# A recurrent (Mamba-style) layer with a quantized FFN on eight cores: the convolution of the next channel block is emitted four steps earlier, and the reload of the gated values gets one semaphore per half

## The chip, the cores and the metric

The kernel runs on all 8 cores of one Trainium2 chip. Each core computes 2 of the 16 sequences by itself; the cores share nothing but the weights they read. The metric is the device time of one execution, in microseconds (us), of the slowest core.

## What is computed

The input x is 16 sequences of 2048 tokens with 1024 channels, in float32. The reference, cut to what matters:

```python
xn = layernorm(x)
xp = xn @ in_proj_w.T + in_proj_b          # 1024 -> 2 * 2048
x1, x2 = split(xp, 2)
u  = silu(causal_depthwise_conv4(x1) + conv_b)
for t in range(2048):                      # per channel d, 16 states n
    h[d, n] = dA[d, n] * h[d, n] + dB[d, n] * u[t, d]
    y[t, d] = sum_n h[d, n] * C[d, n]
s = (y * silu(x2)) @ out_proj_w.T + out_proj_b
g = silu(ffn(xn))                          # silu(gate) * up, then down; hidden 3072, int weights / 127
out = x + s * g
```

## The kernel before

Everything is written out by hand: `build_schedule` appends each instruction to the list of its engine, with the semaphores that it waits for, and each engine runs its list in order. All matrix work is bf16, with PSUM tiles of 128x512. The work of one sequence (loop `u`) has these stages.

1. Layernorm of 16 tiles of 128 tokens, and transposes into `xnt` (channels on partitions, all 2048 tokens).
2. The scan stage: 16 channel blocks (loop `i`), each of 128 channels of the 2048. Each block has 16 steps (loop `n`, one for each state), and then a gate. A document-wide naming is used below: scan n, y n, piece g, unit.
   - Scan n (line 605, VectorE, `bfb<-aa,bfb`, 128x2048) runs the recurrence of state n over all tokens. It writes one of two buffers, so it waits until the y matmuls of step n-2 have read theirs. Behind it stands a small operation (line 613) that builds the diagonal weights C*dB of that state.
   - y n (line 625, TensorE) is 4 matmuls that add the state's part to `ps_y`, four PSUM banks that hold the block's sum. They wait for line 613 of their step.
   - The gate (line 640, VectorE) multiplies `ps_y` by silu(x2) when y 15 is done; SyncE then stores the result to `xg_spill` in DRAM (line 661).
   - Pieces 0 to 7 (`emit_ip_piece`, line 511) are the input projection of the next block, i+1, 8 matmuls each: pieces 0 to 3 give x1, 4 to 7 give x2. Pieces 0 to 5 stand behind y 1, 3, 5, 7, 9 and 11, pieces 6 and 7 behind the gate's place in the program, that is right behind y 15 on TensorE. ScalarE empties them (lines 521 and 532).
   - Three FFN units (`emit_f1`) a block: one ahead of scan 0, one behind y 6, one behind y 12. A unit is 8 transposes of its weight (line 155, emptied by ScalarE at line 162) and 16 matmuls (line 462, emptied at line 475). The one at the block's head comes with the 16 transposes of the next block's input weights (`emit_ip_slabs`), so 24 transposes stand ahead of its matmuls. A short product of VectorE (line 427) belongs to every second unit.
   - The convolution of block i+1 (`emit_conv`): 4 diagonal weights on VectorE (line 554), then 4 groups of 4 matmuls (line 571), emptied by ScalarE with silu (line 580) into the input of the next block's scans. It needs pieces 0 to 3. In the kernel before it is emitted behind y 13. The last block of a sequence (i = 15) has no next block and so neither pieces nor a convolution.
3. Two column halves of 1024 tokens (loop `cb`). In each, SyncE reads the gated values back with 32 DMAs of 128 KB (line 695), 16 for the first 512 columns (p = 0) and 16 for the second (p = 1). The output projection (line 719) has 8 output blocks m, and for each of them a group of 16 matmuls for p = 0 in `ps_a` or `ps_b` and one of 16 for p = 1. Then comes the down projection of the FFN (line 817), with the product and the sum of the outputs. In the second half the first FFN layer (48 units) runs ahead of the output projection.

All the groups of pieces, units, convolution and projections take the two PSUM tiles `ps_a` and `ps_b` in turn. The 48 units of the first half are just the three of each block, so nothing of the FFN is left between the last gate of a sequence and the first output projection. In this kernel one semaphore counts all reload DMAs, and each group of line 719 waits for the last of the 32:

```python
w = [fr, (ts, ev_t), ("qxg", lastl),
     ("sv", ev_g_done_v)]
```

Of the kernel before, what the change touches and what calls it, by code (L numbers as in the profile page):

```python
# [20 lines left out]
NI = DI // 128  # L21
# [11 lines left out]
RACE_CHECK = True  # L33

ENGS = ("sync", "gpsimd", "vector", "scalar", "tensor")
SEMS = ("q0", "qx0", "qx1", "qx2", "qx3", "qxg", "qxp", "qs",
        "qsx0",
        "qip0", "qip1", "qf0", "qf1", "qe0", "qe1", "qd0", "qd1",
        "sv", "ss", "st")
# [194 lines left out]
def build_schedule(sch, dr, sb, ps):  # L234
    op, val = sch.op, sch.val
    f32a, bfa, bfb = sb["f32a"], sb["bfa"], sb["bfb"]
# [5 lines left out]
    for nm_s, nm_d in (("b1s", "b1r"), ("convws", "convw"), ("convbs", "convb"),  # L242
# [6 lines left out]
                      inc="q0", inck=16)  # L249
# [57 lines left out]
    for u in range(BPC):  # L307
# [5 lines left out]
        for g in range(4):  # L313
# [61 lines left out]
            for jj in range(4):  # L375
# [3 lines left out]
                for dc in range(NK):  # L379
                    w = []  # L380
# [209 lines left out]
        for i in range(NI):  # L590
            uslot = bfb[:, 4096 + 2048 * (i % 2):4096 + 2048 * (i % 2) + 2048]
            if i + 1 < NI:
                emit_ip_slabs(i + 1)
            emit_f1(u, 0, 1)
            for n in range(NST):
                hs = bfb[:, 10240 + 2048 * (n % 2):10240 + 2048 * (n % 2) + 2048]
                dg = bfb[:, 2564 + 128 * (n % 2):2564 + 128 * (n % 2) + 128]
                if n >= 2:
                    ev_hfree = ev_dmm[(i, n - 2)]
                elif i > 0:  # L600
                    ev_hfree = ev_dmm[(i - 1, NST + n - 2)]
                else:
                    ev_hfree = bfb_free_st
                ev_scan[(i, n)] = op("vector",
                                     (lambda i, n, hs, uslot: lambda e: e.tensor_tensor_scan(  # L605
                                         hs,
                                         sb["aa"][:, 16 * i + n:16 * i + n + 1].broadcast_to([128, T]),
                                         uslot, 0.0, ALU.mult, ALU.add))(i, n, hs, uslot),
                                     waits=[("ss", ev_usilu[i]),
                                            ("st", ev_hfree)],  # L610
                                     inc="sv")
                ev_dg = op("vector",
                           (lambda i, n, dg: lambda e: e.tensor_scalar_mul(  # L613
                               dg, sb["idbs"][:],
                               sb["cbt"][:, 16 * i + n:16 * i + n + 1]))(i, n, dg),
                           inc="sv")
                lastd = None
                for pc in range(NPC):
                    w = []
                    if pc == 0:  # L620
                        w = [("sv", ev_dg)]
                        if n == 0:
                            w.append(("sv", ev_gate.get(i - 1, 0)))
                    lastd = op("tensor",
                               (lambda n, pc, dg, hs: lambda e: e.matmul(  # L625
                                   ps["y"][:, 512 * pc:512 * (pc + 1)], dg,
                                   hs[:, 512 * pc:512 * (pc + 1)],
                                   start=(n == 0), stop=(n == NST - 1)))(n, pc, dg, hs),
                               waits=w, inc="st" if pc == NPC - 1 else None)
                ev_dmm[(i, n)] = lastd  # L630
                if n % 2 == 1 and n <= 11 and i + 1 < NI:
                    emit_ip_piece(i + 1, n // 2)
                if n in (6, 12):
                    emit_f1(u, 0, 1)
                if n == 13 and i + 1 < NI:
                    emit_conv(i + 1)
            xgs = bfb[:, 16640:18688]
            sx2 = SX2_SLOT[i % 2]
            ev_gate[i] = op("vector",
                            (lambda xgs, sx2: lambda e: e.tensor_tensor(  # L640
                                xgs, ps["y"][:, :], sx2, ALU.mult))(xgs, sx2),
                            waits=[("st", ev_dmm[(i, NST - 1)]),
                                   ("ss", ev_x2evac[(i, NPC - 1)]),
                                   ("qsx0", ev_xgst.get(i - 1, 0))],
                            inc="sv")
            if DEBUG_TAPS and u == 0:
                op("sync",
                   (lambda i, uslot: lambda e: e.dma_start(
                       out=dr["t_u"][128 * i:128 * (i + 1), :], in_=uslot))(i, uslot),
                   waits=[("sv", ev_gate[i])], inc="q0", inck=16)  # L650
                op("sync",
                   (lambda i, sx2: lambda e: e.dma_start(
                       out=dr["t_sx2"][128 * i:128 * (i + 1), :], in_=sx2))(i, sx2),
                   waits=[("sv", ev_gate[i])], inc="q0", inck=16)
                op("sync",
                   (lambda i: lambda e: e.dma_start(
                       out=dr["t_hpp"][128 * i:128 * (i + 1), :],
                       in_=bfb[:, 12288:14336]))(i),
                   waits=[("sv", ev_gate[i])], inc="q0", inck=16)
            ev_xgst[i] = op("sync",  # L660
                            (lambda u, i, xgs: lambda e: e.dma_start(
                                out=dr["xg"][u, 128 * i:128 * (i + 1), :],
                                in_=xgs))(u, i, xgs),
                            waits=[("sv", ev_gate[i])],
                            inc="qsx0", inck=16)
            if i + 1 < NI:
                emit_ip_piece(i + 1, 6)
                emit_ip_piece(i + 1, 7)
# [5 lines left out]
        for cb in range(NCB):  # L674
# [8 lines left out]

            ev_sevac = {}
            ev_emm_last = 0
            lastl = None
            for p in range(2):
                pg = 2 * cb + p
                for k in range(NI):
                    w = []  # L690
                    if p == 0 and k == 0:
                        w = [("qsx0", ev_xg_all0), ("sv", ev_b_end_v),
                             ("st", ev_f2_mm_last)]
                    lastl = op("sync",
                               (lambda u, pg, p, k: lambda e: e.dma_start(
                                   out=bfb[:, 2048 + 8192 * p + 512 * k:
                                           2048 + 8192 * p + 512 * (k + 1)],
                                   in_=dr["xg"][u, 128 * k:128 * (k + 1),
                                                512 * pg:512 * (pg + 1)]))(u, pg, p, k),
                               waits=w, inc="qxg", inck=16)  # L700
            for m in range(8):
                ew = []
                if m == 0:
# [6 lines left out]
                for p in range(2):  # L710
                    idx, fr = rot.acquire()
                    psm = PSR[idx]
                    for k in range(NI):
                        w = []
                        if k == 0:
                            w = [fr, (ts, ev_t), ("qxg", lastl),
                                 ("sv", ev_g_done_v)]
                        lastm = op("tensor",
                                   (lambda m, p, k, psm, wst: lambda e: e.matmul(  # L719
# [186 lines left out]
```

How the kernel before makes its waits and increments, by code:

```python
                def f(eng):  # L71
                    for (w, fn, ih) in ops_:
                        for (h, v) in w:
                            eng.wait_ge(h, v)
                        ins = fn(eng)
                        if ih is not None:
                            assert ins is not None
                            ins.then_inc(ih[0], ih[1])
```

## Time and profile before

| | |
|---|---|
| runs of the kernel, two | 4256.11 and 4409.76 us, median 4332.93 us |
| profiled execution, its own time | 4262.4 us |
| its span on the slowest core (core 4) | 4260.9 us |
| spans of the eight cores | 4232.0 to 4260.9 us |
| TensorE matmuls, busy | 2921.0 us (69%) |
| VectorE busy | 2578.2 us (61%) |
| ScalarE busy | 1165.9 us (27%) |
| mean granted TensorE clock, core 4 | 0.869 |

The span is the time from the first to the last instruction of a core; the execution's own time is 1.5 us longer. Busy shares are means over stages: in the two scan stages VectorE is busy nearly all of the time, in the projections TensorE is. A granted clock of 1.00 is TensorE at 2.4 GHz, 0.50 is 1.2 GHz. A matmul's busy time in a timeline row includes the end of the pipeline, so a row of 8 matmuls of 128x512 shows 1.89 us where the next group starts about 1.7 us behind it.

### The profile page before, as it was taken

The page shows a single profiled execution, that of the slowest core. Times are in us where ns is not written, and L with a number is a line of the kernel's source. Part 1 is how long each engine was busy: PE and PEld are TensorE (multiplying, and loading weights), DVE is VectorE, ACT ScalarE, POOL GpSimd, SP SyncE. Part 2 cuts the span into 40 slices and gives each one's busy share as a digit, 9 for nine tenths or more (in the row PEclk, how much of TensorE's full clock was granted, in tenths as well). Part 3 has the DMA queues.
Part 4 walks back from the last instruction along what each step waited for, and adds up shares of the span by engine and source line. Part 5 has one row for each costly group of instructions (what it writes and reads, how often), then busy time and mean ns, then how long its engine had stood idle before and what let it go on. Part 6 is the DMA issues. An engine that isn't in the chain of part 4 may idle for free.

```text
span 4260.9 us, 40605 instructions; the slowest of 8 cores (4232.0 to 4260.9 us)
## 1 busy us (share of the span) xinstructions
PE 2921.0 (69%) x14080; PEld 1296.0 (30%) x14080; DVE 2578.2 (61%) x1507; ACT 1165.9 (27%) x1575; POOL 169.3 (4%) x324
## 2 busy tenths in 40 slices
PE   3666676677675687767736776776776756877777
PEld 1222222222222343333322222222222223433333
DVE  2999999999998010000129999999999980100001
ACT  6222222122121233432362222221221212334332
POOL 0000000000000000000000000000000000000000
PEclk9889889888887889999958888888888878999998
DMA  3111111111101436323231111111111014263322
GB/s 99 25 20 25 25 20 25 25 20 26 24 15 26 111 62 153 47 48 55 54 109 25 20 25 25 20 25 25 20 27 23 15 27 118 54 156 46 51 50 70
DMA packets 84574, 196.07 MB, mean 46 GB/s; under 512 B 10272, under 2 KB 27040, under 8 KB 84384
## 3 DMA queue, kind: packets, MB, share of 16 engines
q0 software_dynamic: 46080, 109.07, 16.0%
q1 hardware_dynamic: 38304, 84.40, 5.9%
q8 instruction: 127, 2.08, 0.2%
q14 instruction: 63, 0.52, 0.0%
HBM read 268.93 MB, written 33.55 MB: 71 GB/s over the span
## 4 chain that ended last, share of the span: by engine, by line
PE 35%; issue 27%; DVE 23%; ACT 10%; DMA 2%; SPq 1%; DVEq 0%; ACTq 0%; POOLq 0%
DVE bfb L605 19%; PE ps_a L462 7%; PE ps_b L462 6%; PE ps_a L817 5%; ACT bfa L162 4%; PE ps_b L817 4%; PE ps_y L625 3%; PE ps_a L719 3%; PE ps_b L719 3%; DVE bfb L613 2%; PE ps_a L511 2%; ACT bfb L162 2%; PE ps_b L511 2%; ACT f32a L336 1%; ACT s_sb L475 1%
## 5 line engine op out<-in xcount | busy, mean ns | idle before, releaser
L605 DVE TENSOR_TENSOR_SCAN bfb<-aa,bfb 128x2048 bf16<-128x2048 f32 x512 | 2261.0, 4416 | 114.7 <-PE ps_y L625 66.4
L625 PE MATMUL ps_y<-bfb 128*128 128x512 bf16 x2048 | 636.9, 444 | 595.9 <-DVE bfb L613 594.5
L462 PE MATMUL ps_a<-xnt,bfa 128*128 128x512 bf16 x1536 | 404.2, 411 | 247.3 <-ACT bfa L162 226.6
L759 DVE TENSOR_TENSOR bfb<-f32a,s_sb 128x1024 bf16<-128x1024 f32 x32 | 39.2, 1225 | 788.1 <-PE ps_t L155 597.3
L625 PEld LDWEIGHTS ps_y<-bfb 128*128 128x128 bf16 x2048 | 198.9, 107 | 978.2 <-issue 854.3
L462 PE MATMUL ps_b<-xnt,bfa 128*128 128x512 bf16 x1536 | 374.1, 387 | 43.0 <-ACT bfa L162 43.0
L427 DVE TENSOR_TENSOR bfa<-s_sb 128x1024 bf16<-128x1024 bf16 x96 | 65.9, 687 | 514.0 <-ACT s_sb L475 514.0
L162 ACT ACTIVATE bfa<-ps_t 128x1024 bf16<-128x1024 bf16 x320 | 319.0, 1019 | 201.7 <-PE ps_t L155 197.8
L511 PE MATMUL ps_a<-xnt,bfa 128*128 128x512 bf16 x1024 | 321.9, 471 | 2.6 <-ACT bfb L532 1.4
L511 PE MATMUL ps_b<-xnt,bfa 128*128 128x512 bf16 x1024 | 318.7, 467 | 0.0
L462 PEld LDWEIGHTS ps_a<-xnt,bfa 128*128 128x128 bf16 x1536 | 147.0, 102 | 438.7 <-issue 313.0
L475 ACT ACTIVATE s_sb<-ps_a,cnss 128x512 bf16<-128x512 f32 x192 | 131.9, 687 | 446.9 <-PE ps_a L462 444.5
L155 PE MATMUL ps_t<-idbs,bfa 128*128 128x128 bf16 x2560 | 191.4, 224 | 66.3 <-ACT bfa L162 36.6
L462 PEld LDWEIGHTS ps_b<-xnt,bfa 128*128 128x128 bf16 x1536 | 152.5, 100 | 237.2 <-issue 74.9
L817 PE MATMUL ps_a<-bfa,bfb 128*128 128x512 bf16 x768 | 196.8, 419 | 18.5 <-ACT bfb L162 18.5
L155 PEld LDWEIGHTS ps_t<-idbs,bfa 128*128 128x128 bf16 x2560 | 167.5, 100 | 127.3 <-issue 77.1
L719 PE MATMUL ps_a<-bfb,bfa 128*128 128x512 bf16 x512 | 125.6, 402 | 109.2 <-ACT bfa L162 62.5
L475 ACT ACTIVATE s_sb<-ps_b,cnss 128x512 bf16<-128x512 f32 x192 | 131.9, 687 | 248.3 <-PE ps_b L462 248.3
L511 PEld LDWEIGHTS ps_b<-xnt,bfa 128*128 128x128 bf16 x1024 | 121.2, 118 | 190.6 <-issue 121.6
L511 PEld LDWEIGHTS ps_a<-xnt,bfa 128*128 128x128 bf16 x1024 | 119.6, 117 | 186.0 <-issue 113.4
L817 PE MATMUL ps_b<-bfa,bfb 128*128 128x512 bf16 x768 | 171.0, 379 | 0.0
L532 ACT ACTIVATE bfb<-ps_a,b1s 128x512 bf16<-128x512 f32 x64 | 44.0, 687 | 405.6 <-PE ps_a L511 389.3
(60 smaller groups left out, 1786.3 us busy)
## 6 DMA issues: line engine op xcount, KB each, us to landing
f32a<-x SPq DMA_DIRECT2D x64, 512.0 KB, 7.1
bfa<-wg POOLq DMA_DIRECT2D x96, 256.0 KB, 3.6
bfa<-wu POOLq DMA_DIRECT2D x96, 256.0 KB, 3.6
bfb<-wd POOLq DMA_DIRECT2D x32, 768.0 KB, 7.0
bfa<-win POOLq DMA_DIRECT2D x64, 256.0 KB, 5.6
xg_spill<-bfb SPq DMA_DIRECT2D x32, 512.0 KB, 2.6
bfa<-wout POOLq DMA_DIRECT2D x32, 512.0 KB, 6.1
bfb<-xg_spill SPq DMA_DIRECT2D x128, 128.0 KB, 5.6
```

What stands on the lines that cost most here:

```text
L155: (lambda stage, bank, g0, j: lambda e: e.transpose(bank[:, 128 * j:128 * (j + 1)], stage[:, 128 * (g0 + j):128 * (g0 + j + 1)], self.idma ...
L162: (lambda wst, bank, g0, nb: lambda e: e.activation(wst[:, 128 * g0:128 * (g0 + nb)], bank[:, 0:128 * nb], AF.Identity))(wst, bank, g0, nb),
L427: (lambda mh, sl: lambda e: e.tensor_tensor(bfa[:, 8192 + 1024 * mh:8192 + 1024 * (mh + 1)], s_sb[:, 2048 * sl:2048 * sl + 1024], s_sb[:, ...
L462: (lambda wst, k, cb, p, psm: lambda e: e.matmul(psm[:, :], wst[:, 128 * k:128 * (k + 1)], xnt[:, 2048 * k + 1024 * cb + 512 * p: 2048 * k ...
L475: (lambda dst, psm, act: lambda e: e.activation(dst, psm[:, :], act, scale=sb["cnss"][:, 2:3]))(dst, psm, act),
L511: (lambda k, p, psm, wst: lambda e: e.matmul(psm[:, :], wst[:, 128 * k:128 * (k + 1)], xnt[:, 2048 * k + 512 * p:2048 * k + 512 * (p + 1)] ...
L532: (lambda p, mrow, psm, sx2: lambda e: e.activation(sx2[:, 512 * p:512 * (p + 1)], psm[:, :], AF.Silu, bias=sb["b1s"][:, mrow:mrow + 1]))( ...
L605: (lambda i, n, hs, uslot: lambda e: e.tensor_tensor_scan(hs, sb["aa"][:, 16 * i + n:16 * i + n + 1].broadcast_to([128, T]), uslot, 0.0, A ...
L613: (lambda i, n, dg: lambda e: e.tensor_scalar_mul(dg, sb["idbs"][:], sb["cbt"][:, 16 * i + n:16 * i + n + 1]))(i, n, dg),
L625: (lambda n, pc, dg, hs: lambda e: e.matmul(ps["y"][:, 512 * pc:512 * (pc + 1)], dg, hs[:, 512 * pc:512 * (pc + 1)], start=(n == 0), stop= ...
L719: (lambda m, p, k, psm, wst: lambda e: e.matmul(psm[:, :], wst[:, 128 * k:128 * (k + 1)], bfb[:, 2048 + 8192 * p + 512 * k: 2048 + 8192 * ...
L817: (lambda wst, k, p, psm: lambda e: e.matmul(psm[:, :], wst[:, 128 * k:128 * (k + 1)], bfa[:, 8192 + 1024 * k + 512 * p: 8192 + 1024 * k + ...
```

## The change

Two edits. The convolution of the next block is emitted behind piece 4 of step 9 in place of step 13, so that its 4 diagonal weights, 16 matmuls and 4 operations of ScalarE stand four steps earlier in their engines' lists. And the reload DMAs of p = 0 and of p = 1 count on semaphores of their own (`qxg`, `qxg2`); a group of matmuls of line 719 waits for the 16 of its own half alone. Their order on SyncE's queue is the same.

```diff
+SEMS = (..., "qxg", "qxg2", ...)
...
                 if n % 2 == 1 and n <= 11 and i + 1 < NI:
                     emit_ip_piece(i + 1, n // 2)
+                if n == 9 and i + 1 < NI:
+                    emit_conv(i + 1)
                 if n in (6, 12):
                     emit_f1(u, 0, 1)
-                if n == 13 and i + 1 < NI:
-                    emit_conv(i + 1)
...
-            lastl = None
+            lastl_p = [None, None]
...
-                    lastl = op("sync",
+                    lastl_p[p] = op("sync",
...
-                               waits=w, inc="qxg", inck=16)
+                                    waits=w, inc=("qxg" if p == 0 else "qxg2"),
+                                    inck=16)
...
-                            w = [fr, (ts, ev_t), ("qxg", lastl),
+                            w = [fr, (ts, ev_t),
+                                 (("qxg" if p == 0 else "qxg2"), lastl_p[p]),
                                  ("sv", ev_g_done_v)]
```

TensorE's list in the middle of block 2 of the first sequence, before: y 8 and y 9 (the row of 8), piece 4, y 10 and y 11, piece 5, y 12.

```order
L625 MATMUL ps_y<-bfb 128x512 x8
L511 MATMUL ps_a<-xnt,bfa 128x512 x8
L625 MATMUL ps_y<-bfb 128x512 x8
L511 MATMUL ps_b<-xnt,bfa 128x512 x8
L625 MATMUL ps_y<-bfb 128x512 x4
```

The same place in the changed kernel, where line 571 is the convolution:

```order
L625 MATMUL ps_y<-bfb 128x512 x8
L511 MATMUL ps_a<-xnt,bfa 128x512 x8
L571 MATMUL ps_b<-bfb 128x512 x4
L571 MATMUL ps_a<-bfb 128x512 x4
L571 MATMUL ps_b<-bfb 128x512 x4
L571 MATMUL ps_a<-bfb 128x512 x4
L625 MATMUL ps_y<-bfb 128x512 x8
L511 MATMUL ps_b<-xnt,bfa 128x512 x8
L625 MATMUL ps_y<-bfb 128x512 x4
```

The 16 matmuls of the convolution now stand between piece 4 and y 10, so that y 10 comes behind 24 matmuls instead of 8.

TensorE's list at the end of the same block, before: the unit behind y 12 (line 462), y 13, the convolution, y 14 and y 15, pieces 6 and 7.

```order
L462 MATMUL ps_a<-xnt,bfa 128x512 x8
L462 MATMUL ps_b<-xnt,bfa 128x512 x8
L625 MATMUL ps_y<-bfb 128x512 x4
L571 MATMUL ps_a<-bfb 128x512 x4
L571 MATMUL ps_b<-bfb 128x512 x4
L571 MATMUL ps_a<-bfb 128x512 x4
L571 MATMUL ps_b<-bfb 128x512 x4
L625 MATMUL ps_y<-bfb 128x512 x8
L511 MATMUL ps_a<-xnt,bfa 128x512 x8
L511 MATMUL ps_b<-xnt,bfa 128x512 x8
```

The same place in the changed kernel:

```order
L462 MATMUL ps_a<-xnt,bfa 128x512 x8
L462 MATMUL ps_b<-xnt,bfa 128x512 x8
L625 MATMUL ps_y<-bfb 128x512 x12
L511 MATMUL ps_a<-xnt,bfa 128x512 x8
L511 MATMUL ps_b<-xnt,bfa 128x512 x8
```

Between the unit and pieces 6 and 7 TensorE has only y 13, y 14 and y 15, one behind each scan. The last block of a sequence has the rows `x12` there in both kernels.

VectorE's list in the middle of that block, before: scan 9 to scan 11 (line 605), each with its diagonal of line 613.

```order
L605 SCALAR_TENSOR_TENSOR bfb<-aa,bfb 128x2048
L613 TENSOR_SCALAR bfb<-idbs,cbt 128x128
L605 SCALAR_TENSOR_TENSOR bfb<-aa,bfb 128x2048
L613 TENSOR_SCALAR bfb<-idbs,cbt 128x128
L605 SCALAR_TENSOR_TENSOR bfb<-aa,bfb 128x2048
```

The same in the changed kernel, where line 554 is the convolution's diagonals:

```order
L605 SCALAR_TENSOR_TENSOR bfb<-aa,bfb 128x2048
L613 TENSOR_SCALAR bfb<-idbs,cbt 128x128
L554 TENSOR_SCALAR bfb<-idbs,convws 128x128 x4
L605 SCALAR_TENSOR_TENSOR bfb<-aa,bfb 128x2048
L613 TENSOR_SCALAR bfb<-idbs,cbt 128x128
```

The four small operations stand ahead of scan 10 now, and no longer ahead of scan 14.

## Rows read from the trace of the kernel before

**Rows 1.** The costliest groups, shapes kept apart: the scans (busy us, mean ns | idle before).

```profile
L605 DVE TENSOR_TENSOR_SCAN bfb<-aa,bfb 128x2048 bf16<-128x2048 f32 x512 | 2261.0, 4416 | 114.7 <-PE ps_y L625 66.4 <-PE ps_t L155 24.3 <-ACT bfb L580 23.9
```

**Rows 2.** The table of waits: who waited for whom, us in total, times, longest.

```profile
DVE bfb L605 <- PE ps_y L625: 66.4, 30, 4.0
...
DVE bfb L640 <- PE ps_y L625: 46.9, 32, 2.3
PE ps_a L719 <- DMA bfb<-xg_spill: 46.7, 2, 23.7
```

**Rows 3.** Timeline of block 5, from scan 10 to y 10 (start, us, engine).

```profile
551.81 4.42 DVE L605 TENSOR_TENSOR_SCAN bfb<-aa,bfb 128x2048 bf16<-128x2048 f32 x1
...
552.04 1.86 PE L625 MATMUL ps_y<-bfb 128*128 128x512 bf16 x4 [3.45 <-DVE bfb L613]
...
553.70 3.62 PE L511 MATMUL ps_a<-xnt,bfa 128*128 128x512 bf16 x8
...
556.28 4.42 DVE L605 TENSOR_TENSOR_SCAN bfb<-aa,bfb 128x2048 bf16<-128x2048 f32 x1
...
557.11 1.36 PE L625 MATMUL ps_y<-bfb 128*128 128x512 bf16 x4
```

**Rows 4.** Stretches with granted clock: length, PE, PEld, DVE, ACT, POOL busy, PEclk, DMA share, GB/s.

```profile
552.00:557.50 5.50, 5.46 (x13) 1.90 (x14) 5.50 (x3) 0.03 (x1) 0.00 (x0) 0.50 0.00 0
571.80:580.80 9.00, 6.76 (x31) 2.75 (x30) 7.61 (x4) 3.33 (x5) 0.00 (x0) 1.00 0.00 1
...
1370.50:1374.90 4.40, 1.87 (x4) 0.44 (x4) 2.24 (x2) 0.00 (x0) 1.05 (x2) 0.50 0.06 7
```

**Rows 5.** Timeline of block 5, from the diagonals of the convolution to the gate.

```profile
569.72 0.73 DVE L554 TENSOR_SCALAR bfb<-idbs,convws 128x128 bf16<-128x128 bf16 x4
...
571.80 1.03 PE L625 MATMUL ps_y<-bfb 128*128 128x512 bf16 x4
...
572.66 1.03 PE L571 MATMUL ps_a<-bfb 128*128 128x512 bf16 x4
...
576.65 1.03 PE L625 MATMUL ps_y<-bfb 128*128 128x512 bf16 x4
...
579.55 1.02 PE L625 MATMUL ps_y<-bfb 128*128 128x512 bf16 x4 [1.88 <-DVE bfb L613]
...
580.82 2.29 DVE L640 TENSOR_TENSOR bfb<-ps_y,bfb 128x2048 bf16<-128x2048 f32 x1 [1.41 <-PE ps_y L625]
```

**Rows 6.** Timeline of block 15 of the first sequence, which has no convolution in its tail.

```profile
1366.07 1.02 PE L625 MATMUL ps_y<-bfb 128*128 128x512 bf16 x4 [0.39 <-DVE bfb L613]
...
1370.55 1.87 PE L625 MATMUL ps_y<-bfb 128*128 128x512 bf16 x4 [3.45 <-DVE bfb L613]
...
1372.66 2.29 DVE L640 TENSOR_TENSOR bfb<-ps_y,bfb 128x2048 bf16<-128x2048 f32 x1 [2.26 <-PE ps_y L625]
```

**Rows 7.** Timeline behind the gate of block 5: piece 6, FFN unit, third scan.

```profile
580.41 1.89 PE L511 MATMUL ps_a<-xnt,bfa 128*128 128x512 bf16 x8
...
588.22 3.33 PE L462 MATMUL ps_a<-xnt,bfa 128*128 128x512 bf16 x8 [1.48 <-DVE bfb L613]
...
594.49 4.42 DVE L605 TENSOR_TENSOR_SCAN bfb<-aa,bfb 128x2048 bf16<-128x2048 f32 x1 [1.82 <-PE ps_y L625]
```

**Rows 8.** Timeline behind the gate of block 4: piece 6, first y, third scan.

```profile
499.72 3.57 PE L511 MATMUL ps_a<-xnt,bfa 128*128 128x512 bf16 x8
...
514.25 1.89 PE L625 MATMUL ps_y<-bfb 128*128 128x512 bf16 x8
...
515.38 4.42 DVE L605 TENSOR_TENSOR_SCAN bfb<-aa,bfb 128x2048 bf16<-128x2048 f32 x1 [4.01 <-PE ps_y L625]
```

**Rows 9.** Timeline where the output projection begins, in the first and the second sequence.

```profile
1384.34 16.29 SPq L695 DMA_DIRECT2D bfb<-xg_spill  x32
...
1405.59 6.33 PE L719 MATMUL ps_a<-bfb,bfa 128*128 128x512 bf16 x16 [23.74 <-DMA bfb<-xg_spill]
...
3534.12 5.32 PE L719 MATMUL ps_a<-bfb,bfa 128*128 128x512 bf16 x16 [22.92 <-DMA bfb<-xg_spill]
```

More of the change, by code:

```diff
@@ L35 @@
 ENGS = ("sync", "gpsimd", "vector", "scalar", "tensor")
-SEMS = ("q0", "qx0", "qx1", "qx2", "qx3", "qxg", "qxp", "qs",
+SEMS = ("q0", "qx0", "qx1", "qx2", "qx3", "qxg", "qxg2", "qxp", "qs",
         "qsx0",
@@ L693, in build_schedule @@
                              ("st", ev_f2_mm_last)]
-                    lastl = op("sync",
[L695 to L699, printed above, removed]
-                               waits=w, inc="qxg", inck=16)
+                    lastl_p[p] = op("sync",
+                                    (lambda u, pg, p, k: lambda e: e.dma_start(
+                                        out=bfb[:, 2048 + 8192 * p + 512 * k:
+                                                2048 + 8192 * p + 512 * (k + 1)],
+                                        in_=dr["xg"][u, 128 * k:128 * (k + 1),
+                                                     512 * pg:512 * (pg + 1)]))(u, pg, p, k),
+                                    waits=w, inc=("qxg" if p == 0 else "qxg2"),
+                                    inck=16)
             for m in range(8):
```

## The prediction

> **What bounds the kernel now.** I read the groups of costly instructions first. The 512 scans take 2261.0 us, 4.416 each, and VectorE sits idle before them for 114.7 us in all [rows 1]. That is more than half of the span of 4260.9 us, so in the scan stages the scans are the bound, and only idle time of VectorE there can be won or added. The reader is to see three waits in the 114.7: 66.4 for y matmuls, and 24.3 and 23.9 that occur once each, at the head of each sequence. They sum to 114.6. So no scan within a sequence waits for the convolution's output (line 580): it is ready in time at step 13 already, and having it earlier buys nothing.
>
> The table of waits says how the 66.4 us fall: 30 times, 4.0 us at most, 2.2 on average [rows 2]. There are 30 blocks with a successor (15 in each sequence). By the timelines it is nearly always the third scan behind a gate, which must wait for y 0, and y 0 stands behind pieces 6 and 7, 24 transposes and a unit. The gates wait 46.9 us for y 15 in 32 times. The output projection waits twice for the reload, 23.7 us at most.
>
> Then I read timelines around one block with the granted clock beside them, since TensorE's list is what is moved. Three things are to be seen:
>
> - Where TensorE has had only a few matmuls behind each scan, it is slow when work comes: y 9 takes 1.86 us for 4 matmuls and piece 4 runs from 553.70 to about 557.1 [rows 3]; the clock in these 5.5 us is 0.50, TensorE at 1.2 GHz [rows 4].
> - With the convolution between y 13 and y 14, TensorE is busy for 6.76 of the 9.0 us ahead of the gate, the clock is 1.00 [rows 4], y 15 takes 1.02 us, and the gate waits 1.41 us [rows 5].
> - In block 15, which has no convolution there, the y 14 still takes 1.02 us, but y 15 takes 1.87 us at a clock of 0.50, and the gate waits 2.26 us [rows 4, 6]. It has the very order (y 13, y 14, y 15 in a row) that the change gives to the 30 other blocks.
>
> **The change part by part.**
>
> *The tail loses its matmuls.* Between the unit and the pieces there are now 12 matmuls spread over three scans. The nearest rows are those of block 15: 2.26 - 1.41 = 0.85 us more at each gate [rows 5, 6], on the path, since gate and scans follow each other on one engine. 30 x 0.85 = 25.5 us. The other end is 0, if in most blocks the unit and y 13 come late enough to keep the clock up to y 15. I take 25.5, since a row with the same order shows it.
>
> *Pieces 6 and 7 start at the lower clock.* They follow y 15 at once. At 2.4 GHz piece 6 shows 1.89 us and the third scan waits 1.82 us, although half of the unit is slow there [rows 7]. Where piece 6 began at the lower clock it took 3.57 us and the third scan waited 4.01 us, the longest of all [rows 8, 2]. If every block goes that way, the wait rises from the mean of 2.2 by 1.8, 30 x 1.8 = 54 us; if the clock is back as soon as the pieces start, it rises by 0. By the row of 5.5 us at 0.50, y 15 uses 1.7 of such a stretch and up to 3.8 are left for the pieces, which costs 1.9; some stretches will be shorter. I take 1.0 us a block, a little over the middle, 30 us. What hides nothing here: the two scans between gate and third scan (9.0 us) are already overrun by 2.2.
>
> *The convolution stands ahead of y 10.* Scan 12 writes the buffer that y 10 reads, so y 10 is due before it. Scan 10 starts at 551.81 in this block, now some 0.6 later because of the diagonals (0.73 us on VectorE, as long as they took ahead of scan 14, so no term of its own) [rows 3, 5]. Scan 12 is then due at 552.4 + 2 x 4.48 = 561.4, 4.48 being a scan with its issue (556.28 - 551.81) [rows 3]. TensorE: piece 4 gives way at 557.1, the 16 matmuls take 576.65 - 572.66 = 4.0 at 2.4 GHz [rows 5], so y 10 starts at 561.1, and a scan starts 1.13 behind the start of its y (515.38 - 514.25) [rows 8]: 562.2. Scan 12 would wait 0.8 us here. With the clock up from y 9 on, y 9 and piece 4 take half of the 5.06 us, y 10 starts at 558.6, and nothing waits. So the ends are 0 and 30 x 0.8 = 24 us. Only the blocks with a whole slow stretch before y 10 pay, and I take 0.3 a block, 9 us. The far end is a convolution wholly at 1.2 GHz, 4 us more, which the rows speak against: TensorE is busy without a break from y 9 on, and in the row y 10 at 557.11 is already faster (1.36 for 4) than y 9.
>
> *Other queues.* On ScalarE four operations move ahead of the emptying of piece 5 and of the unit; it is idle for most of a block, and the PSUM tiles alternate as before. The x1 columns that the convolution reads come from piece 3, two steps earlier. SyncE and GpSimd keep their order. These I cost at 0; the cover is ScalarE's idle time.
>
> *The reload.* The 32 loads are issued over 16.29 us; the matmuls start at 1405.59, after 23.74 us idle [rows 9]. The sixteenth is issued about 8 us before the last, so the p = 0 group can start near 1397.4. It took 6.33 us (5.32 in the second sequence), part of it at the lower clock [rows 9]. The p = 1 group still needs the last load, so it begins at about 1405.5 in place of some 6 us later. The gain is at most what p = 0 took, 6.3 + 5.3 = 11.6 us for both. The pause before p = 1 may leave the clock down; its 16 matmuls would then lose about 16 x 0.21 = 3.4 us each time, by the two speeds of piece 6, and 4.8 us stay. I take 8. In the second column half the matmuls wait for no load, the table has two such waits alone [rows 2], so 0 there.
>
> *The sum.* 25.5 + 30 + 9 - 8 = 56.5 us on the profiled execution's own time of 4262.4 us: 4319 us, +1.3%. That execution agrees with the faster of the two runs shown (4256.11), while their median, 4332.93, lies between two runs that are 3.6% apart. My number is to be read beside 4256 to 4262.
>
> A rule that speaks against the clock terms: the Trainium skill, "TensorE: Matmul & The Clock Gate", section on the HAM clock gate (Part 1), says that for modelling the ramp penalty is below 1% of a typical kernel's span. By it, as an estimate, the two clock terms together would be under 42.6 us and the time 4306 us at most. The trace goes against it as a rule for this kernel: the waits of the third scans alone are 66.4 us, 1.6% of the span, and the spread from 1.82 to 4.01 among them follows the clock of the pieces.
>
> **The rivals.**
>
> *A: the lower clock in full, in every block.* Mechanism: every gate comes after a lean tail, y 15 and the pieces all run at 1.2 GHz, and scan 12 waits in every block as well. 25.5 + 54 + 24 - 5 = +98.5 us, 4361 us, +2.3%. For it: both blocks 15 look alike, and the phases of blocks repeat, so that one bad pattern can stay. Against it: time at the lower clock spent on y 15 can't be spent on the pieces too, and in this trace most blocks have their pieces at 2.4 GHz. It is slower than before beyond 2% from about 3.1 us a block on (85 + 8 = 93 over 30).
>
> *B: the tail keeps its clock.* Without the convolution at 13 the unit behind y 12, which itself may be slow and end late, covers enough of the tail. Then only the reload counts: 4262.4 - 8 = 4254 us. For it: y 14 of block 15 is still fast. Against it: y 15 of block 15 is not.
>
> *C: the pattern of clock falls well.* The matmuls of y 9, piece 4, convolution and y 10 are one busy run, and blocks shift so that the units behind the gate run fast. If the third scans waited for nothing: -66.4 - 8 = -74 us, 4188 us, -1.7%. Against it: y 0 still has 24 transposes and 32 matmuls before it, and the one mechanism that the change touches there works the other way. Beyond 2% it would need the gates' wait to shrink too, which they can't, since y 15 follows scan 15.
>
> **How the numbers follow.** Forecast 0.55, A 0.25, B 0.15, C 0.05. The time is that of the forecast, 4319 us. The range: B gives 4254, with 11.6 us of gain for the reload 4250; A gives 4361, and if a few blocks' scan 12 waits twice as long as in my row, 15 us more, 4376, rounded to 4380. So 4250 to 4380. About 2% (85 us) is what a measurement of this kernel tells from no change. Slower by more: A, 0.25. Faster by more: a corner of C, 0.02. Within 2%: 0.73.
>
> **What would show it.** In the changed profile: idle before the gate 1.4 us if the tail keeps its clock, near 2.3 if not, in total about 72 us where 46.9 stood. Third scans: a total near 96 us where 66.4 stood. Waits of scan 12 on y matmuls: new, about 9 us, none in blocks whose y 9 took 1.0. PEclk near 1.00 for the convolution at step 9 and 0.50 ahead of the gates. The reload: the first matmul of line 719 waits some 15 us in place of 23, and a new short wait of about 2 us stands before its second group. I am wrong if the gates stay at 1.4, if a scan other than the third and scan 12 begins to wait (scan 15 on y 13 is the candidate, if the unit behind y 12 is slow), or if the loads of p = 0 land no earlier than those of p = 1.

## The result, and the profile after

The changed kernel is slower: the ratio to the kernel before is 1.0177, with a 95% interval of 1.0163 to 1.0191. The profiled execution took 4330.78 us, with spans of 4306.9 to 4329.2 us on the eight cores; that is 68 us above the profiled execution of before, 4262.4 us, which was itself 5 us above the median that the ratio goes by; the ratio stands for 75 us. Over all executions the medians are 4339.96 us (11) and 4306.46 us (10); some executions of either kernel have the cores of a die at a lower clock for a while and take 2 to 6% longer, so only undisturbed ones are compared here.

The page of the changed kernel, its parts on busy time and clock:

```profile
PE 2953.8 (68%) x14080; PEld 1310.6 (30%) x14080; DVE 2581.7 (60%) x1507; ACT 1167.1 (27%) x1575; POOL 169.3 (4%) x324
...
PEclk9888888888887899999968888888888878999999
...
L605 DVE TENSOR_TENSOR_SCAN bfb<-aa,bfb 128x2048 bf16<-128x2048 f32 x512 | 2261.5, 4417 | 165.0 <-PE ps_y L625 118.5
```

VectorE is busy for 3.5 us longer than before, TensorE for 32.8 us longer with the same 14080 matmuls. The scans cost the same within a nanosecond (4417 ns against 4416), but VectorE's idle time ahead of them has gone from 114.7 us [rows 1] to 165.0. The table of waits of the changed kernel (us in total, times, longest):

```profile
DVE bfb L605 <- PE ps_y L625: 118.5, 67, 3.7
...
DVE bfb L640 <- PE ps_y L625: 70.9, 32, 2.3
```

Against [rows 2]: scans wait 118.5 us for y matmuls where it was 66.4, +52.1, and 67 times where it was 30; gates wait 70.9 where it was 46.9, +24.0. That makes 76 us. The reload gives back about 10 (below), and the two heads of sequences cost 1.7 less (46.5 against 48.2). 76 - 10 - 2 = 64 of the 68 us lie in these places.

One block of the changed kernel shows every step. Its timeline from y 9 to the next third scan, block 5 of the first sequence (gate at 597.95):

```profile
565.68 1.86 PE L625 MATMUL ps_y<-bfb 128*128 128x512 bf16 x4 [3.46 <-DVE bfb L613]
...
567.33 3.62 PE L511 MATMUL ps_a<-xnt,bfa 128*128 128x512 bf16 x8
...
570.75 1.18 PE L571 MATMUL ps_b<-bfb 128*128 128x512 bf16 x4
...
575.23 1.89 PE L625 MATMUL ps_y<-bfb 128*128 128x512 bf16 x8
576.37 4.42 DVE L605 TENSOR_TENSOR_SCAN bfb<-aa,bfb 128x2048 bf16<-128x2048 f32 x1 [1.23 <-PE ps_y L625]
...
576.96 1.89 PE L511 MATMUL ps_b<-xnt,bfa 128*128 128x512 bf16 x8
...
585.04 3.39 PE L462 MATMUL ps_a<-xnt,bfa 128*128 128x512 bf16 x8 [1.41 <-ACT bfa L162]
...
589.99 1.89 PE L625 MATMUL ps_y<-bfb 128*128 128x512 bf16 x8
...
591.12 4.42 DVE L605 TENSOR_TENSOR_SCAN bfb<-aa,bfb 128x2048 bf16<-128x2048 f32 x1 [1.23 <-PE ps_y L625]
...
595.84 1.87 PE L625 MATMUL ps_y<-bfb 128*128 128x512 bf16 x4 [3.96 <-DVE bfb L613]
...
597.50 3.62 PE L511 MATMUL ps_a<-xnt,bfa 128*128 128x512 bf16 x8
...
597.95 2.29 DVE L640 TENSOR_TENSOR bfb<-ps_y,bfb 128x2048 bf16<-128x2048 f32 x1 [2.26 <-PE ps_y L625]
...
607.43 1.89 PE L462 MATMUL ps_a<-xnt,bfa 128*128 128x512 bf16 x8 [1.48 <-ACT bfa L162]
...
612.01 4.42 DVE L605 TENSOR_TENSOR_SCAN bfb<-aa,bfb 128x2048 bf16<-128x2048 f32 x1 [2.21 <-PE ps_y L625]
```

The reader is to see four waits in brackets. y 9 and piece 4 run slowly, as they did in [rows 3]; the convolution follows, y 10 starts at 575.23, and scan 12 waits 1.23 us. The unit behind y 12 (585.04) takes 3.39 us for 8 matmuls, y 13 starts at 589.99 and scan 15 waits 1.23. y 15 takes 1.87 us and the gate waits 2.26. Piece 6 takes 3.62 us, and the third scan of the next block waits 2.21. The granted clock in these stretches (columns as in [rows 4]):

```profile
567.00:571.00 4.00, 4.00 (x11) 1.43 (x10) 4.00 (x3) 0.00 (x0) 0.00 (x0) 0.50 0.00 0
571.00:576.00 5.00, 4.56 (x20) 1.64 (x19) 4.13 (x2) 3.20 (x5) 0.00 (x0) 1.00 0.00 0
...
581.00:588.00 7.00, 5.51 (x20) 2.42 (x21) 7.00 (x3) 1.02 (x1) 0.53 (x1) 0.52 0.28 39
588.00:595.00 7.00, 3.88 (x18) 1.60 (x16) 5.77 (x3) 1.38 (x2) 0.00 (x0) 0.99 0.00 0
595.00:602.00 7.00, 6.16 (x16) 2.23 (x17) 4.74 (x5) 0.69 (x1) 0.00 (x0) 0.52 0.14 56
```

0.50 or 0.52 where the matmuls are slow, 1.00 or 0.99 between. In this block y 9, the unit at 585.04 and y 15 with piece 6 each follow a stretch in which TensorE had only y matmuls or transposes, and each ran at 1.2 GHz. It is not so every time: the unit at 607.43 also has 24 transposes right before it and takes 1.89 us.

Added up over the timelines of all blocks, the waits for y matmuls split by step as follows (before, changed):

| waits, us (times) | before | changed |
|---|---|---|
| third scan (n = 2) | 65.2 (28) | 80.8 (29) |
| scan 12 | 0 | 19.1 (17) |
| scan 15 | 0 | 15.9 (15) |
| gate | 46.9 (32) | 70.9 (32) |

Waits of under 0.3 us are left out of the first three rows, and so is scan 9 (0.9 us before, 1.8 in the changed kernel), so they sum to a little less than the table of waits.

The timelines of all 32 blocks also say which of TensorE's groups were slow. Waits of scan 12 over 1 us stand in 15 blocks, and they are the ones in which y 9 (1.86 us) and piece 4 (3.5 to 3.6 us) were both slow; in the others it waits 0.33 us at most. Scan 15 waits in 15 blocks, and they are the 15 in which the unit behind y 12 takes 3.3 to 3.6 us for its first 8 matmuls; in the trace before that unit takes 1.89 us in all 32.

The reload, in the changed kernel:

```profile
1425.70 16.28 SPq L695 DMA_DIRECT2D bfb<-xg_spill  x32
...
1438.36 5.12 PE L721 MATMUL ps_a<-bfb,bfa 128*128 128x512 bf16 x16 [15.24 <-DMA bfb<-xg_spill]
...
1447.15 5.30 PE L721 MATMUL ps_b<-bfb,bfa 128*128 128x512 bf16 x16 [3.66 <-DMA bfb<-xg_spill]
...
1455.36 3.61 PE L721 MATMUL ps_a<-bfb,bfa 128*128 128x512 bf16 x16 [2.02 <-ACT bfa L162]
```

The first group waits 15.24 us in place of 23.74 [rows 9], and the second one has a wait of its own of 3.66 us. From the first load to the second output block (1425.70 to 1455.36) it is 29.7 us; in the trace before it was 1384.34 to 1418.29, 34.0 us. In the second sequence it is 27.2 against 32.7. So 4.3 and 5.5 us are gained, 9.8 in all.

### The profile page after: what moved, and what is told of

Its sections match the earlier page's. It is cut to its first block, busy times and chain, and to the rows that moved or that the text cites. A ratio compares the mean times of both kernels' runs of the same rounds, so it can differ in the third digit from the quotient of the medians.

```text
span 4329.2 us, 40605 instructions; the slowest of 8 cores (4306.9 to 4329.2 us)
## 1 busy us (share of the span) xinstructions
PE 2953.8 (68%) x14080; PEld 1310.6 (30%) x14080; DVE 2581.7 (60%) x1507; ACT 1167.1 (27%) x1575; POOL 169.3 (4%) x324
## 4 chain that ended last, share of the span: by engine, by line
PE 43%; issue 24%; DVE 18%; ACT 11%; DMA 2%; SPq 1%; DVEq 0%; ACTq 0%; POOLq 0%
DVE bfb L605 15%; PE ps_a L462 8%; PE ps_b L462 6%; PE ps_y L625 6%; ACT bfa L162 5%; PE ps_a L819 4%; PE ps_a L511 4%; PE ps_b L819 4%; PE ps_a L721 3%; PE ps_b L721 3%; PE ps_b L511 2%; DVE bfb L613 2%; ACT bfb L162 2%; PE ps_t L155 1%; PE ps_a L571 1%
## 5 line engine op out<-in xcount | busy, mean ns | idle before, releaser
L605 DVE TENSOR_TENSOR_SCAN bfb<-aa,bfb 128x2048 bf16<-128x2048 f32 x512 | 2261.5, 4417 | 165.0 <-PE ps_y L625 118.5
L462 PE MATMUL ps_a<-xnt,bfa 128*128 128x512 bf16 x1536 | 420.5, 423 | 246.6 <-ACT bfa L162 246.6
L462 PE MATMUL ps_b<-xnt,bfa 128*128 128x512 bf16 x1536 | 367.9, 383 | 43.0 <-ACT bfa L162 43.0
L511 PE MATMUL ps_a<-xnt,bfa 128*128 128x512 bf16 x1024 | 349.9, 503 | 2.4 <-ACT bfb L532 1.4
L511 PE MATMUL ps_b<-xnt,bfa 128*128 128x512 bf16 x1024 | 293.1, 438 | 0.0
L462 PEld LDWEIGHTS ps_a<-xnt,bfa 128*128 128x128 bf16 x1536 | 150.3, 105 | 449.8 <-issue 332.1
L155 PE MATMUL ps_t<-idbs,bfa 128*128 128x128 bf16 x2560 | 201.4, 230 | 66.7 <-ACT bfa L162 36.8
L155 PEld LDWEIGHTS ps_t<-idbs,bfa 128*128 128x128 bf16 x2560 | 176.6, 104 | 133.9 <-issue 88.4
L511 PEld LDWEIGHTS ps_a<-xnt,bfa 128*128 128x128 bf16 x1024 | 128.3, 126 | 212.0 <-issue 158.7
```

What stands on the lines that cost most here:

```text
L155: (lambda stage, bank, g0, j: lambda e: e.transpose(bank[:, 128 * j:128 * (j + 1)], stage[:, 128 * (g0 + j):128 * (g0 + j + 1)], self.idma ...
L462: (lambda wst, k, cb, p, psm: lambda e: e.matmul(psm[:, :], wst[:, 128 * k:128 * (k + 1)], xnt[:, 2048 * k + 1024 * cb + 512 * p: 2048 * k ...
L511: (lambda k, p, psm, wst: lambda e: e.matmul(psm[:, :], wst[:, 128 * k:128 * (k + 1)], xnt[:, 2048 * k + 512 * p:2048 * k + 512 * (p + 1)] ...
L605: (lambda i, n, hs, uslot: lambda e: e.tensor_tensor_scan(hs, sb["aa"][:, 16 * i + n:16 * i + n + 1].broadcast_to([128, T]), uslot, 0.0, A ...
```

## The experiments

The edits of e3, e6, e7 and e8 are shown against the changed kernel, those of e1, e2 and e9 against the kernel before, those of e5 against e2 and of e10 against e5. My theory after this: the whole loss is in the scan stage and comes by TensorE's clock, which the convolution at step 13 had held up. The rivals: that the order of the list itself makes it (24 matmuls ahead of y 10), and that the second edit has a share.

**e1 and e9: the convolution at step 9, nothing else.**

```diff
+                if n == 9 and i + 1 < NI:
+                    emit_conv(i + 1)
...
-                if n == 13 and i + 1 < NI:
-                    emit_conv(i + 1)
```

> The kernel before with the convolution at step 9 and nothing else (one semaphore for the reload). Theory: the lean tail and the late y 10 make all of the loss, so gates wait about 71 us, third scans 80, scan 12 about 19, scan 15 about 16, and the time is some 75 to 85 us above before (ratio 1.018 to 1.020), that is the changed kernel plus the 8 us that the split reload gives. Rival: the split reload costs time (its extra wait, or DMA order), and then this kernel is faster than the changed one.

Measured: ratio 1.0222, with an interval of 1.0114 to 1.0329, too wide to set it against 1.0177. Its profile has the expected waits before scans and gates (115.5 and 71.6 us). So the same kernel was run again:

> The same kernel as e1 (convolution at step 9 alone, one reload semaphore), run again because e1's interval was wide. Theory: ratio 1.0195, between 1.018 and 1.021, that is the changed kernel's 1.0177 plus the 0.2% that the split reload gives. Rival: at or below 1.0177, so that the two edits don't simply add.

Measured: 1.0192 (1.0175 to 1.0208). Its table of waits:

```profile
DVE bfb L605 <- PE ps_y L625: 115.3, 66, 3.7
...
DVE bfb L640 <- PE ps_y L625: 71.3, 32, 2.3
...
PE ps_a L719 <- DMA bfb<-xg_spill: 47.0, 2, 23.9
```

Scans and gates wait as in the changed kernel (115.3 and 71.3 us), and the reload's 47.0 us are back. The convolution's place makes the whole loss. The intervals of 1.0192 and 1.0177 overlap (that of e9 begins at 1.0175, that of the changed kernel ends at 1.0191), so that the two edits add is likely by the rows and not shown by the ratios.

**e2: the split reload, nothing else.**

```diff
+SEMS = (..., "qxg", "qxg2", ...)
...
+                            w = [fr, (ts, ev_t),
+                                 (("qxg" if p == 0 else "qxg2"), lastl_p[p]),
```

> The kernel before with the split reload and nothing else. Theory: -8 us, between -4.8 and -11.6 (ratio 0.998), the first matmul of line 719 waits about 15 us in place of 23, and a wait of some 2 us stands before its second group. Rival: within noise, 0, if the loads of p = 0 land no earlier or the clock eats the gain; the scan stages are as before in both (66 us before third scans, 47 before gates).

Measured: 0.9965 (0.9928 to 1.0001), with medians of 4247 us against 4256, 9 us less. The interval just reaches 1; the rows say where the gain lies:

```profile
DVE bfb L605 <- PE ps_y L625: 63.0, 28, 4.0
...
DVE bfb L640 <- PE ps_y L625: 47.0, 32, 2.3
...
PE ps_a L721 <- DMA bfb<-xg_spill: 32.8, 2, 17.4
...
PE ps_b L721 <- DMA bfb<-xg_spill: 3.4, 2, 3.1
```

The scan stage waits as before (63.0 and 47.0). The first groups wait 32.8 us for the reload in place of 46.7, the second ones 3.4.

**e3: the tail filled.** The changed kernel with 16 matmuls behind y 13 whose result nothing reads. They repeat the convolution's operands, so TensorE's list from y 13 to the gate reads as before, but they do no work of the layer.

```diff
                 if n in (6, 12):
                     emit_f1(u, 0, 1)
+                if n == 13 and i + 1 < NI:
+                    for _ in range(4):
+                        fidx, ffr = rot.acquire()
+                        fps = PSR[fidx]
+                        for kk in range(4):
+                            fl = op("tensor", ... e.matmul(fps[:, :],
+                                        bfb[:, 2052 + 128 * kk:2052 + 128 * (kk + 1)],
+                                        bfb[:, 512 * p + kk:512 * p + kk + 512], ...)
+                        rot.release(fidx, "st", fl)
+                    ev_convmm[i + 1] = fl
```

In the cut call `p` is the loop's `_`. The last line makes the next diagonal weights wait for these matmuls, which read the old ones.

> The changed kernel with the 16 matmuls of the convolution repeated behind y 13, into the two PSUM tiles in turn, and never read: extra work that computes nothing. Theory (the tail's loss is TensorE's clock): ahead of the gate the granted clock is 1.00 again, gates wait 1.4 us each (47 us in all, not 71), third scans about 66 us, and the time falls by 35 to 50 us against the changed kernel, to 4285 us or so; scan 12 keeps its 10 to 20 us. Rival (the loss comes from the new order of the list, not from the clock): gates stay at 2.26 us or the 480 extra matmuls only cost, and the time is that of the changed kernel or above, 4330 us or more.

Measured: 1.0039 (1.0002 to 1.0075); 480 more matmuls make the changed kernel 1.4% faster, some 58 us. The gate rows:

```profile
DVE bfb L605 <- PE ps_y L625: 93.5, 68, 3.9
...
DVE bfb L655 <- PE ps_y L625: 48.3, 32, 2.3
```

Line 655 is the gate here. Block 5 again, the stretch ahead of the gate and y 15:

```profile
582.00:588.80 6.80, 6.30 (x30) 2.73 (x29) 4.57 (x2) 0.69 (x1) 0.00 (x0) 1.00 0.00 0
...
587.87 1.02 PE L625 MATMUL ps_y<-bfb 128*128 128x512 bf16 x4 [0.50 <-DVE bfb L613]
```

The clock is 1.00 there and y 15 takes 1.02 us, as it does in 27 of the 30 blocks with a filled tail. Gates wait 48.3 us, as before the change. Split by step the scans wait 46.5 us (third), 24.7 (scan 12) and 18.4 (scan 15). The rival that the order alone makes the gates' loss is out: all the layer's work stands in the order of the changed kernel, and that loss is gone. The gain was larger than I expected, since the third scans fell below their value before, too. What stays is 43 us at scan 12 and scan 15, which this experiment doesn't explain.

**e6: every gap filled.** The changed kernel with such empty matmuls (identity weights on `xnt`) behind y 8, y 11, y 12 and y 13.

```diff
+                if n in (8, 11, 12) and i + 1 < NI:
+                    emit_fill(2 if n == 8 else 1)
                 if n == 9 and i + 1 < NI:
                     emit_conv(i + 1)
                 if n in (6, 12):
                     emit_f1(u, 0, 1)
+                if n == 13 and i + 1 < NI:
+                    emit_fill(4)
```

> The changed kernel with matmuls that compute nothing (identity weights, never read) behind y 8 (8), y 11 (4), y 12 (4) and y 13 (16). Theory (waits of scan 12 and scan 15 come from the lower clock on piece 4 and on the unit behind y 12, not from the place of the convolution as such): those waits, 24.7 and 18.4 us with the tail filled alone, go to under 8 us each, gates stay at 47, and the time falls to 4250 us or less, below before. Rival (24 matmuls ahead of y 10 are too many at any clock, and the filling only lengthens the queue): scan 12 keeps 20 us or more and the time is 4270 us or above.

Measured: 4245.07 us in the profiled execution, the only one that can be compared, so there is no ratio; the kernel before had 4253.81 us at the least beside it.

```profile
DVE bfb L619 <- PE ps_y L639: 61.2, 31, 3.1
...
DVE bfb L658 <- PE ps_y L639: 46.7, 32, 2.3
```

Of the 61.2 us left before scans the timelines put 56.8 at the third scan; scan 12 never waits, and scan 15 does once, for 2.5 us, in the last block, which has no filling. In all 30 filled blocks y 9 takes 1.02 us, piece 4 1.89 and the unit behind y 12 1.89. So 24 matmuls between y 9 and y 10 are not too many at 2.4 GHz, and both new waits of the change come from the slow stretches ahead of them: 35 us in the changed kernel, 2.5 here. Which of the fillings does what was not tried one by one. The third scans still wait 56.8 us with pieces 6 and 7 at full speed in every block; the unit ahead of them is slow in 24 of the 30. The time is that of e2, where the convolution stands at step 13 without fillings (median 4247 us). What step 13 would give with the same fillings was not run.

**e7: the convolution in two halves,** two groups behind piece 4 and two behind y 13.

```diff
-        def emit_conv(i):
+        def emit_conv(i, part=range(4)):
...
+                    emit_conv(i + 1, range(0, 2))
...
+                if n == 13 and i + 1 < NI:
+                    emit_conv(i + 1, range(2, 4))
```

> The changed kernel with the convolution cut in two: the diagonals and two groups (8 matmuls) behind piece 4 in step 9, the other two groups behind y 13. Theory: 8 matmuls in the tail are enough to keep TensorE's clock for y 15 in most blocks, and 16 in place of 24 ahead of y 10 end its lateness, so gates wait 47 to 55 us, scan 12 under 5, scan 15 under 8 and third scans 60 to 70; 4250 to 4270 us. Rival (only a tail with 16 matmuls holds the clock): gates at 65 or more and third scans at 75 or more, 4290 us or above.

Measured: 1.0056 (1.0035 to 1.0078), and

```profile
DVE bfb L605 <- PE ps_y L625: 82.1, 31, 4.1
...
DVE bfb L642 <- PE ps_y L625: 57.9, 32, 2.3
```

Half of the expectation held: scan 12 waits nothing and scan 15 only 1.4 us. But the gates wait 57.9 us, and third scans 78.7 us, where 60 to 70 were expected; the median is 4282 us, above the 4250 to 4270 expected. With 8 matmuls in the tail y 15 takes 1.0 to 1.1 us in 12 blocks, 1.9 in 9 and something between in 9. The timeline has both kinds of block: a gate wait of 2.26 us in one, behind a third scan that waited 3.95, and 1.42 in the next but one. Halving the convolution is worse than the whole of it at step 13 (e2, 0.9965); against the filled tail of e3 (1.0039) the intervals overlap.

**e4 and e5: the unit behind y 0.** The convolution at step 13 again, the split reload, and the unit that stood ahead of scan 0 moved behind y 0.

```diff
                 emit_ip_slabs(i + 1)
-            emit_f1(u, 0, 1)
...
-                if n in (6, 12):
+                if n in (0, 6, 12):
                     emit_f1(u, 0, 1)
```

> The convolution at step 13 as before, the split reload kept, and the unit at a block's head emitted behind y 0 instead of ahead of scan 0. Theory: y 0 then stands behind pieces 6 and 7 and 16 transposes alone, so the 66 us before third scans go to under 10, with nothing new behind it because y 1 is due 4.5 us later than y 0: 4256 - 66 - 8 = 4185 us, ratio 0.983. Rival: the wait moves to the fourth scan (y 1 stands behind the unit, 24 matmuls' worth of time and its transposes), half or more of the 66 us comes back, 4215 us or more; or the clock falls behind the pieces and gates wait more.

Measured: 4204.4 us in the one execution that can be compared. The same kernel once more, for a ratio:

> The same kernel as e4 (convolution at step 13, split reload, unit behind y 0), run again so that it has enough executions for a ratio. Its one look gave 4204 us with 21.6 us left before scans and 48.6 before gates. Theory: ratio 0.987 to 0.989. Rival: that look was a lucky one and the ratio is 0.993 or above.

Measured: 0.9877 (0.9843 to 0.991). y 0 no longer stands behind 32 matmuls and a unit's transposes:

```profile
DVE bfb L639 <- PE ps_y L624: 47.7, 32, 2.3
...
DVE bfb L604 <- PE ps_y L624: 18.5, 17, 2.0
```

Of the 66.4 us before scans 18.5 are left, nearly all at the fourth scan: it waits in 16 blocks, the ones in which the unit behind y 0 begins slowly (3.3 to 3.6 us for 8 matmuls). The first expectation was 4185 us; the rival had its share too, as more than a quarter of the wait moved on. About 0.3% of the gain is the split reload (e2, 0.9965); the intervals of e2 and e5 lie apart, so moving the unit gains by itself.

**e8: the unit behind y 0 in the changed kernel.**

```diff
                 emit_ip_slabs(i + 1)
-            emit_f1(u, 0, 1)
...
-                if n in (6, 12):
+                if n in (0, 6, 12):
                     emit_f1(u, 0, 1)
```

> The changed kernel (convolution at step 9) with the unit at the block's head behind y 0, as in e4. Theory (the losses are separate terms): third scans lose nothing any more, gates still wait 71 us, scan 12 and scan 15 still 35 us together, so the time is e4's 4204 plus 24 plus 35, 4263 us. Rival (the slow pieces 6 and 7 still push something late, now the fourth scan): 20 us or more remain before the fourth scan and the time is 4280 us or above.

Measured: 0.9952 (0.9931 to 0.9974), a median of 4240 us and not the 4263 expected.

```profile
DVE bfb L639 <- PE ps_y L624: 71.7, 32, 2.3
...
DVE bfb L604 <- PE ps_y L624: 28.4, 48, 2.5
```

The gates wait their 71.7 us. But scan 12 waits 8.1 us in all, in 29 short waits of 0.6 us at most (3.3 us by the measure of the table above, which leaves out those under 0.3), and scan 15 4.9 us, in the last block of each sequence, where the changed kernel had 35 together. So the terms are not separate. In e8 y 9 and piece 4 are slow in all 30 blocks, but piece 4 only for a part (at most 3.0 us and not 3.6), and the unit behind y 12 is slow in none of them: with the head's unit moved, the slow stretches fall elsewhere in a block. Against e5, the same but for the convolution's place, step 9 costs 0.0075 of the time, 32 us, 24 of them at the gates and 10 before scans.

**e10: e5 with the gap ahead of y 0 filled,** 8 empty matmuls behind the head's 16 transposes.

```diff
                 emit_ip_slabs(i + 1)
+                emit_fill(2)
```

> The kernel of e4 and e5 with 8 matmuls that compute nothing between the 16 transposes of the block's head and y 0. Theory: what e5 still waits for (18.5 us before scans, nearly all the fourth) comes from the unit at the lower clock behind the transposes; with the gap filled it goes under 6 us and the time to 4185 to 4190 us, ratio 0.984. Rival: the fill costs 1.7 us of TensorE in each block and gives no clock back; the waits stay at 15 us or more and the time is 4200 us or above.

Measured: 0.984 (0.9821 to 0.9858), the profiled execution 4187.97 us.

```profile
DVE bfb L654 <- PE ps_y L639: 47.5, 32, 2.3
...
DVE bfb L619 <- PE ps_y L639: 6.2, 4, 2.4
```

Scans wait 6.2 us in place of 18.5, and the unit behind y 0 begins slowly in 3 blocks in place of 16. The intervals of e10 and e5 overlap, but no execution of e10 that can be compared (4187.3 to 4188.0 us) comes near those of e5 (4199.7 to 4220.5); the kernel before had medians of 4255 and 4259 us beside them. The waits of the scan stage are now the gates' 47.5 us, which is the time of y 15 itself, and the two heads of sequences. This version beats the kernel before by 1.6% and the changed one by 3.3%. e5 does most of it (1.2%) without the empty matmuls.

## Why the prediction was right or wrong

The time forecast, 4319 us (+1.3%), is 12 us below the profiled execution, and the range and the side of each term held: the reload gains, everything in the scan stage loses. The ratio, 1.0177, leaves no doubt of a loss, and the cost terms of the prediction (64.5 us) were eight times its gain, so a loss should have been said outright and not as "within 2%". That the sum came so close is in part luck: one term was 14 us too high, two others together 26 us too low. By terms:

- **The tail loses its matmuls: right.** Forecast +25.5 us from block 15's rows, measured +24.0 (70.9 against 46.9). e3 shows the cause: with matmuls in the tail it is +1.4. Block 15 was the right row, as it had the order of the changed kernel already.
- **Pieces 6 and 7 at the lower clock: the pieces right, their wait twice too large.** Forecast +30, measured +15.6 at third scans (80.8 against 65.2). Added up over the 30 blocks, the two pieces take 156 us where they took 125, so 31 us more, just as priced; piece 6 is slow in all 30 blocks where it was in 7. What I missed is the unit behind them. It takes 143 us where it took 156: in 12 of the 30 blocks it begins at full speed (607.43 above, 1.89 us, where in [rows 7] it took 3.33), in 4 before. I priced the pieces on top of a mean wait that already held a slow unit in 26 blocks, and 13 of the 31 us came back there. The two do come together in the other 18 blocks, which wait up to 3.7 us.
- **The convolution ahead of y 10: twice too small.** Forecast +9, measured +19.1. The wait where it occurs is 1.23 us and not 0.8, because the four groups took 4.48 us (570.75 to 575.23) and not 4.0; and it exceeds 1 us in 15 blocks, where 9 us are 11 waits of 0.8. Why the groups take half a microsecond longer at step 9 is open; they do so in blocks with a fast y 9 and piece 4, too. e6 shows that the slow y 9 and piece 4 are the cause of the wait, as the walk had it.
- **Scan 15 on y 13: not in the sum.** I named it as the candidate that would make me wrong, and priced it at nothing. It is +15.9 us, 2.5 of them in the last block, whose own order the change leaves alone. The unit behind y 12 ran at a clock of 0.52. In the trace before the slow stretch lay ahead of it, on piece 5, and was over when the unit came:

```profile
561.40:564.60 3.20, 3.20 (x9) 1.03 (x7) 3.20 (x1) 0.00 (x0) 0.00 (x0) 0.50 0.01 3
...
562.49 2.94 PE L511 MATMUL ps_b<-xnt,bfa 128*128 128x512 bf16 x8
...
568.35 1.89 PE L462 MATMUL ps_a<-xnt,bfa 128*128 128x512 bf16 x8 [1.41 <-ACT bfa L162]
```

  In the changed kernel y 10 came so late that y 11 and piece 5 followed it without a break, all at full speed (575.23 and 576.96 above); then TensorE idled for 2.2 us, and y 12, the transposes and the unit ran at the lower clock. In block 5 the slow stretch thus lies on the unit and not on piece 5. What puts it there is open: in 6 of the 15 blocks with a wait of scan 12 over 1 us, so with a y 10 as late, the unit runs at full speed. e6, with the idle stretches filled, takes the wait away and doesn't single out a step.

- **The reload: right.** Forecast -8, between -4.8 and -11.6; the timelines show -9.8, and e2 some 9 us in an interval that just reaches none.
- **The edits at no cost: right.** No row of ScalarE, GpSimd or SyncE stands ahead of a scan in the changed trace beyond the heads of sequences.

So the mechanism, TensorE's clock, was right, and the step that failed is the sizing of three places that follow it: scan 15 put at nothing (15.9 us), scan 12 at 9 us (19.1), and the third scans at 30 us (15.6), because the units' share was left out. In all 24.0 + 15.6 + 19.1 + 15.9 = 74.6 us where the sum had 64.5. Rival A is out: its terms for the scan stage sum to 103.5 us, and the third scans lost 15.6 us, not 54. B is out by the gates' rows, C by the third scans. The Trainium skill's rule, in "TensorE: Matmul & The Clock Gate", Part 1, that for modelling the ramp penalty is under 1% of a typical kernel's span, stands there beside counts of slow matmuls at a kernel's start; taken for the whole of this kernel, as the prediction took it, it would have allowed 42.6 us. This case's runs go against that: empty matmuls alone brought the changed kernel from 4330.78 to 4245.07 us (e6), 2.0%. The prediction's own argument against it, that third scans wait 1.6% of the span, was too strong, since they wait 1.8 us with the pieces at full speed, too [rows 7].

## What to carry to other kernels

When one engine sets the pace and TensorE serves it in small portions, matmuls that are nobody's bottleneck may still do a job: they keep TensorE at 2.4 GHz for the few that are waited for. Before moving such work away, ask what runs last before the next wait, and look in the profile for a place (here the last block) that already has the new order. Here the wait that came once per block went for the most part when the long work was moved behind the short one that is waited for (e5, 0.9877, against e2, 0.9965). Splitting the moved work in two halves (e7) took back two thirds of the change's loss and left 0.6%.

## What the runs showed of the hardware that I had not expected

Adding matmuls that compute nothing made the kernel faster three times: 16 a block in e3 (1.0177 to 1.0039), 32 in e6 (4330.78 to 4245.07 us), 8 in e10 (0.9877 to 0.984, with intervals that overlap; scans wait 6.2 us in place of 18.5). And the clock's slow stretches in blocks of some 80 us form patterns that repeat: the third scans of the kernel before wait 1.8, 2.2, 1.5 and 4.0 us in turn over much of a sequence. An edit elsewhere in the block moves the pattern: y 9 is slow in 17 of 30 blocks before and in 16 of the changed kernel, and in all 30 once the head's unit is moved (e8), while the unit behind y 12 is slow in none, 14 and none. So a term read from one block and multiplied by 30 was good to a factor of two (+30 against +15.6, +9 against +19.1), except where the block's end fixed it (+25.5 against +24.0).
